# A DLRM tower on one core: the last group's layers in two halves, the weights in pieces, the third layer in two strips, and the pair moves shared out anew

## The chip, the cores and the metric

The kernel runs on 1 core of a Trainium2 chip. The metric is the time of one execution on the device in microseconds (us), as the median of the runs. Engines are named as the profile names them: PE is TensorE's matmuls and PEld its weight loads, DVE is VectorE, ACT ScalarE, POOL GpSimd and SP SyncE. SPq, ACTq and POOLq stand for DMA instructions that the engine issues.

## The reference, cut to what matters

A batch of 2048 rows. Each row looks up 27 embeddings of 128 floats in 27 tables, takes the inner product of every pair (351 of them), appends 16 dense inputs, and runs three dense layers (367 to 512 to 256 to 1).

```python
e = jnp.stack([tbl_0[ids[:, 0]], ..., tbl_26[ids[:, 26]]], axis=1)
xactions = jnp.einsum('bfd,bgd->bfg', e, e)
z = xactions[:, _TRIL_I, _TRIL_J].reshape(B, -1)
h = jnp.concatenate([z, dense_ctx], axis=1)
h = jnp.maximum(h @ W_top1 + b_top1, 0.0)
h = jnp.maximum(h @ W_top2 + b_top2, 0.0)
y = h @ W_top3
```

The tables have 1000, 1250, 12500 or 125000 rows. All arrays are float32.

## The kernel before

**Groups and tiles.** The batch is cut into 16 tiles of 128 rows, and two tiles make a group: 8 groups of 256 columns (`COLS`), numbered 0 to 7 (`LAST` is 7). In each group the embeddings come in two ways. The ten smallest tables ("hot") stay in SBUF, split into two float32r parts, and are looked up by matmuls with one-hot columns that DVE builds (L654; PE at L441 and L442, 180 matmuls a group). The other 17 tables ("cold") are gathered row by row by POOL's indirect DMAs (L402), one for each tile and table: 34 a group, 272 in all. PE transposes what they bring (L424, 17 a tile, in five batches of 4, 4, 4, 4 and 1). Both ways fill one of four PSUM banks `fill_ps`, and ACT moves each bank into `et` (cold L551, hot L563).

**Pairs.** For every row of the batch one small matmul (L458, 26x26, two instructions of PE each) gives the row's inner products. Four rows at a time lie in four column strips of PE. A group has four banks of 64 rows, `("pairs", g, 0)` to `("pairs", g, 3)`: banks 0 and 1 are its first tile, banks 2 and 3 its second. They alternate between two PSUM banks `pair_ps`, so bank n waits until bank n-2 has been moved out. `move_pairs` (L343) moves a bank with 16 copies: DVE takes strips 0 and 1 and ACT strips 2 and 3, so 8 copies each, and each engine counts what it moved on a semaphore of its own (`pair_moved_v`, `pair_moved_a`).

**z.** The copies put most pair products where the first layer reads them (`zt`, 3 chunks of 128 rows). Those of the 14 lower features and the dense inputs are placed by 15 small DMAs in `complete_zt` (L313, the dense one L309). In groups 0 to 6 SP issues all 15 after bank 3 of the group was moved.

**Layers.** layer1 (L471) is 12 matmuls of 256 columns, in 24 instructions of PE since a float32 matmul takes two; ACT applies bias and relu (L570). layer2 is 8 matmuls (L497, 16 instructions), in two halves m of 4, with relu at L575. layer3 is 2 matmuls with one weight column (L504); DVE copies the result to `y_row` (L661) and SP stores it (L363).

**Order.** `order()` (L77 to L92) lists the steps, and PE, ACT, DVE and SP each walk that list. For group g above 0, with b = g-1: the first hot fill, layer3 of b-1, pairs 2 and 3 of b among the hot fills, then the rest of the fills, layer1 of b, pairs 0 and 1 of g, and layer2 of b between them. So a group's layers run under the next group's fills. At a hot step DVE builds the one-hots of the hot step after it. At `("layer3", b)` DVE waits for PE and copies y, and SP waits for that copy, stores y and only then goes on to the next ids (`hot_ids`, L331) and to the next z.

**The end.** After the list there is nothing left to run under. PE runs 10 matmuls whose result is not used (`WARM`, L523), then `layer1_last` (L486) on 256 columns, chunk by chunk in the order 2, 1, 0, each chunk when its z has landed; of the last group's 15 moves SP issues 9 (chunk 2 first) and POOL 6. Then follow layer2, layer3, the y copy and the store.

**The start.** ACT issues the weights (L537, L538: 768 and 512 KB, and the vectors at L539) after it has moved group 0's last hot fill; the first layer waits for all three.

## Time and profile before

| what | us |
|---|---|
| median of 3 runs | 396.18 |
| lowest and highest of the 3 | 391.86 and 401.06 |
| the profiled execution, its own time | 398.12 |
| its span, first to last instruction | 396.2 |

The profile is of one execution: what it shows is read against 398.12, of which 1.9 lie around the span. A row of the timeline gives the start, the duration of the stretch, the engine, the line, the operation with its tiles and shapes and the count; in brackets stands how long the engine was idle before it and what ended that. The granted TensorE clock (PEclk) is 1.00 at 2.4 GHz and 0.50 at 1.2 GHz; its mean is 0.974 here.

### The profile page before, as it was taken

The page shows a single profiled execution, that of the slowest core. Times are in us where ns is not written, and L with a number is a line of the kernel's source. Part 1 is how long each engine was busy: PE and PEld are TensorE (multiplying, and loading weights), DVE is VectorE, ACT ScalarE, POOL GpSimd, SP SyncE. Part 2 cuts the span into 40 slices and gives each one's busy share as a digit, 9 for nine tenths or more (in the row PEclk, how much of TensorE's full clock was granted, in tenths as well). Part 3 has the DMA queues.
Part 4 walks back from the last instruction along what each step waited for, and adds up shares of the span by engine and source line. Part 5 has one row for each costly group of instructions (what it writes and reads, how often), then busy time and mean ns, then how long its engine had stood idle before and what let it go on. Part 6 is the DMA issues. An engine that isn't in the chain of part 4 may idle for free.

```text
span 396.2 us, 14625 instructions
## 1 busy us (share of the span) xinstructions
PE 353.3 (89%) x6180; PEld 321.6 (81%) x6180; DVE 264.3 (67%) x1044; ACT 212.2 (54%) x435; POOL 280.2 (71%) x286
## 2 busy tenths in 40 slices
PE   0876859999999969999999999999899999999677
PEld 0776849998789858998889888998799788997465
DVE  2999956992689454993779647992689457933310
ACT  3456273655647481563837483755447382746612
POOL 4887777777877777777777778777777777776030
PEclk9998968999999998999999999999999999999989
DMA  7984453224132522225232522234222422221000
GB/s 271 360 255 135 99 188 84 56 72 149 48 77 61 165 57 58 73 64 157 57 83 59 162 58 76 50 107 121 55 78 61 112 52 55 58 64 51 3 13 2
DMA packets 19602, 37.71 MB, mean 95 GB/s; under 512 B 6793, under 2 KB 8401, under 8 KB 19537
## 3 DMA queue, kind: packets, MB, share of 16 engines
q0 software_dynamic: 8896, 17.89, 17.2%
q1 hardware_dynamic: 8704, 16.00, 12.6%
q10 hardware_dynamic: 1936, 2.89, 2.2%
q8 instruction: 49, 0.80, 0.9%
q14 instruction: 17, 0.13, 0.1%
HBM read 35.88 MB, written 0.01 MB: 91 GB/s over the span
## 4 chain that ended last, share of the span: by engine, by line
PE 64%; POOL 16%; issue 7%; DMA 6%; SPq 3%; DVE 3%; ACT 2%; ACTq 0%
PE fill_ps L441 16%; PE fill_ps L442 16%; POOL rows L402 16%; PE pair_ps L458 10%; PE mlp_ps L471 7%; PE mlp_ps L497 6%; PE fill_ps L424 5%; DMA rows<-tbl_d,ids_sb 3%; SPq L313 3%; PE mlp_ps L504 2%; PE fill_ps L486 2%; DVE work L343 1%; DMA work<-work 1%; ACT et L551 1%; DMA ids_sb<-ids_d 1%
## 5 line engine op out<-in xcount | busy, mean ns | idle before, releaser
L402 POOL DMA_INDIRECT rows<-tbl_d,ids_sb x272 | 276.3, 1016 | 86.5 <-issue 80.2
L441 PE MATMUL fill_ps<-one_hot,table_hi 128*128 128x256 f32 x720 | 183.8, 294 | 14.1 <-DVE one_hot L654 14.1
L442 PE MATMUL fill_ps<-one_hot,table_lo 128*128 128x256 f32 x720 | 178.9, 288 | 0.0
L654 DVE TENSOR_SCALAR one_hot<-hot_ids 128x256 fp32r<-128x256 f32 x720 | 166.7, 303 | 13.1 <-PE fill_ps L442 12.3
L441 PEld LDWEIGHTS fill_ps<-one_hot,table_hi 128*128 128x128 f32 x720 | 141.8, 197 | 16.0 <-issue 14.0
L442 PEld LDWEIGHTS fill_ps<-one_hot,table_lo 128*128 128x128 f32 x720 | 141.9, 197 | 0.2
L343 DVE COPY work<-pair_ps 26x112 f32<-26x112 f32 (+1 forms) x256 | 66.0, 258 | 90.0 <-PE pair_ps L458 86.8
L343 ACT COPY work<-pair_ps 26x112 f32<-26x112 f32 (+1 forms) x256 | 61.2, 239 | 84.2 <-PE pair_ps L458 81.5
L551 ACT COPY et<-fill_ps 128x512 f32<-128x512 f32 (+1 forms) x80 | 79.4, 1118 | 0.5
L563 ACT COPY et<-fill_ps 128x512 f32<-128x512 f32 x40 | 46.7, 1225 | 41.4 <-PE fill_ps L442 34.4
L458 PEld LDWEIGHTS pair_ps<-et 128*26 128x26 f32 x4096 | 46.2, 104 | 25.4 <-issue 16.1
L458 PE MATMUL pair_ps<-et 128*26 128x26 f32 x4096 | 55.7, 193 | 12.0 <-issue 5.9
L424 PE MATMUL fill_ps<-ident,rows 128*128 128x128 f32 x272 | 39.5, 282 | 11.0 <-DMA rows<-tbl_d,ids_sb 10.9
L424 PEld LDWEIGHTS fill_ps<-ident,rows 128*128 128x128 f32 x272 | 30.8, 143 | 13.6 <-DMA rows<-tbl_d,ids_sb 12.9
L471 PE MATMUL mlp_ps<-work,w_sb 128*128 128x256 f32 x168 | 37.7, 381 | 1.5 <-DMA work<-work 0.9
L471 PEld LDWEIGHTS mlp_ps<-work,w_sb 128*128 128x128 f32 x168 | 31.4, 190 | 6.3 <-issue 1.3
L497 PE MATMUL mlp_ps<-work,w_sb 128*128 128x256 f32 x128 | 31.5, 392 | 0.0
L497 PEld LDWEIGHTS mlp_ps<-work,w_sb 128*128 128x128 f32 x128 | 24.2, 198 | 2.9
L570 ACT ACTIVATE work<-mlp_ps,vectors 128x256 f32<-128x256 f32 x28 | 11.8, 471 | 23.6 <-PE mlp_ps L471 23.6
L641 DVE TENSOR_SCALAR hot_ids<-hot_ids,first_row 128x512 f32<-128x512 int32 (+1 forms) x48 | 21.2, 455 | 4.0 <-DMA hot_ids<-ids_hot_d 4.0
L661 DVE COPY y_row<-mlp_ps 1x256 f32<-1x256 f32 x8 | 3.3, 412 | 19.6 <-PE mlp_ps L504 19.6
L544 ACT CAST table_hi<-work 128x1024 fp32r<-128x1024 f32 (+1 forms) x8 | 9.3, 1163 | 8.0 <-DMA work<-tbl_d 8.0
(22 smaller groups left out, 62.8 us busy)
## 6 DMA issues: line engine op xcount, KB each, us to landing
hot_ids<-ids_hot_d SPq DMA_DIRECT2D x34, 256.0 KB, 3.8
rows<-tbl_d,ids_sb POOLq DMA_INDIRECT x272, 2.5
work<-tbl_d SPq DMA_DIRECT2D x4, 640.0 KB, 4.3
work<-tbl_d SPq DMA_DIRECT2D x4, 512.0 KB, 7.1
hot_ids<-ids_hot_d ACTq DMA_DIRECT2D x6, 256.0 KB, 8.9
w_sb<-w_d ACTq DMA_DIRECT2D x1, 768.0 KB, 5.4
w_sb<-tbl_d SPq DMA_DIRECT2D x1, 640.0 KB, 4.1
w_sb<-tbl_d SPq DMA_DIRECT2D x1, 512.0 KB, 11.7
```

The source lines that it names most:

```text
L343: last = copy(pair_cols[STRIP * q:STRIP * q + PAIR_COLS, place(q + 1)[1]:, at:at + BANK_ROWS], frm[:, q::STRIPS, :])
L402: nc.gpsimd.indirect_dma_start(out=rows[:, t, c, :], out_offset=None, in_=tables[f], in_offset=bass.IndirectOffsetOnAxis(ap=ids_sb[:, tile ...
L424: last = nc.tensor.transpose(bank[:, c * P:(c + 1) * P], rows[:, t, c0 + c, :], ident[:, :])
L441: nc.tensor.matmul(to, table_hi[:, CHUNK_AT[k] + c, :], hot, start=(c == 0), stop=False)
L442: last = nc.tensor.matmul(to, table_lo[:, CHUNK_AT[k] + c, :], hot, start=False, stop=(c == CHUNKS_OF[k] - 1))
L458: last = nc.tensor.matmul(pair_ps[bank % 2][32 * s:32 * s + PAIR_COLS, r * PAIR_COLS:(r + 1) * PAIR_COLS], et[:, row, 0:FEATURES - 1], et[ ...
L471: last = nc.tensor.matmul(mlp_psum(m), w1_sb[:, c, m * P:(m + 1) * P], zt[:, c, :], start=(c == 0), stop=(c == CHUNKS - 1))
L497: last = nc.tensor.matmul(mlp_ps[m][:, 0:COLS], w2_sb[:, c, m * P:(m + 1) * P], h1[:, c, :], start=(c == 0), stop=(c == K2 - 1))
L551: nc.scalar.copy(et[:, t * P:(t + 1) * P, c0:c0 + n].rearrange("p r f -> p f r"), fill_ps[FILL[step] % FILL_RING][:, 0:n * P].rearrange("p ...
L563: nc.scalar.copy(et[:, :, slot:slot + n].rearrange("p r f -> p f r"), fill_ps[FILL[step] % FILL_RING][:, 0:n * COLS].rearrange("p (f r) -> ...
L641: nc.vector.tensor_scalar(ids.bitcast(F32), ids, first_row[:, n:n + 1], None, ALU.subtract).then_inc(hot_ids_local, 1)
L654: last = nc.vector.tensor_scalar(one_hot[:, (first + c - c0) % ONE_HOT_RING, :], ids, float(c), None, ALU.is_equal)
```

## The change

Five edits:

1. **The last group in two halves.** The layers of group 7 run for its first tile (128 columns) and then for its second. z of the first tile is placed as soon as its banks 0 and 1 are moved, 8 moves issued by SP and 7 by POOL; z of the second after bank 3, 5 moves each by SP, POOL and ACT (`lows_by`). PE's order is layer1 of half 0, layer2 of half 0, layer1 of half 1, layer3 of half 0, layer2 and layer3 of half 1. The 10 unused matmuls go.
2. **Order at the end.** The second half of layer2 of group 6 comes after bank 2 of group 7, no longer before it; layer3 of group 6 comes after bank 3.
3. **Weights in pieces and later.** w1 is loaded in 3 pieces after the first three cold fills of tile 1 of group 0, w2 in 2 pieces, and the vectors, after hot fills 2 and 3 of group 1.
4. **layer3 in two strips** for groups 0 to 6: 4 matmuls of 128 columns, written to two column strips of PE, and two y copies of 128 columns. DVE makes them after it has moved bank 3 of the next group, no longer at the step `layer3`. SP's store stays where it was in its list, ahead of that group's z.
5. **Pair moves.** In groups 0 to 6 ACT moves all of bank 2 (16 copies) and DVE none of it. In group 7 DVE moves all of bank 1 and ACT none. Waits on moved banks count with `moved_through`.

The diff, cut to its core:

```diff
             steps += hot[4:] + cold[0][4:] + [("layer1", b), ("pairs", g, 0)] + cold[1][:2]
-            steps += [("layer2", b, 0), ("pairs", g, 1)] + cold[1][2:] + [("layer2", b, 1)]
-    return steps + [("pairs", GROUPS - 1, 2), ("layer3", GROUPS - 2), ("pairs", GROUPS - 1, 3)]
+            steps += [("layer2", b, 0), ("pairs", g, 1)] + cold[1][2:]
+            if g < LAST:
+                steps.append(("layer2", b, 1))
+    return steps + [("pairs", LAST, 2), ("layer2", LAST - 1, 1), ("pairs", LAST, 3), ("layer3", LAST - 1)]
...
+def strips_of(engine, g, bank):
+    alone = {("dve", 1): range(STRIPS), ("act", 1): range(0)} if g == LAST else {
+        ("act", 2): range(STRIPS), ("dve", 2): range(0)}
+    shared = range(2) if engine == "dve" else range(2, STRIPS)
+    return tuple(alone.get((engine, bank), shared))
...
+def lows_by(engine, t):
+    movers = (("sp", "pool"), ("sp", "pool", "act"))[t]
+    return ALL_LOWS[movers.index(engine)::len(movers)]
...
-        y_ps = mlp_ps[0][0:1, COLS:2 * COLS]
+        y_ps = [mlp_ps[0][STRIP * t:STRIP * t + 1, COLS:COLS + P] for t in range(GROUP_TILES)]
+        y_last_ps = [pair_ps[t][0:1, 0:P] for t in range(GROUP_TILES)]
...
 (SP)
+                elif step == ("pairs", LAST, 1):
+                    complete_zt(sp, LAST, 0, P, lows_by("sp", 0), z_last_in[0])
+                elif step == ("pairs", LAST, PAIR_BANKS - 1):
+                    complete_zt(sp, LAST, P, COLS, lows_by("sp", 1), z_last_in[1])
                 elif step[0] == "layer3":
                     store(step[1])
-            complete_zt(sp, LAST, lows_of(2), z_last_in[2])
-            complete_zt(sp, LAST, SP_LAST_0, z_in)
...
 (PE)
+            def layer1_last(t):
+                pe.wait_ge(z_last_in[t], 16 * (Z_MOVES - len(lows_by("pool", t))))
+                pe.wait_ge(z_last_by_pool[t], 16 * len(lows_by("pool", t)))
+                for m in range(K2):
+                    for c in range(CHUNKS):
+                        last = nc.tensor.matmul(fill_ps[m][:, t * P:(t + 1) * P], w1_sb[:, c, m * P:(m + 1) * P],
+                                                zt[:, c, t * P:(t + 1) * P], start=(c == 0), stop=(c == CHUNKS - 1))
+                    last.then_inc(h1_full, 1)
...
             def layer3(g):
                 for c in range(M2):
                     pe.wait_ge(h2_done, g * M2 + c + 1)
-                    last = nc.tensor.matmul(y_ps, w3_sb[:, c:c + 1], h2[:, c, :],
+                    for t in range(GROUP_TILES):
+                        last = nc.tensor.matmul(y_ps[t], w3_sb[:, c:c + 1], h2[:, c, t * P:(t + 1) * P],
+                                                start=(c == 0), stop=(c == M2 - 1))
...
-            for _ in range(WARM):
-                nc.tensor.matmul(mlp_ps[1][:, 0:COLS], w2_sb[:, 0, 0:P], h1[:, 0, :], start=True, stop=True)
-            layer1_last()
+            pe.wait_ge(fill_moved, len(FILL))
+            layer1_last(0)
             pe.wait_ge(y_done, LAST)
-            for m in range(M2):
-                layer2(LAST, m)
-            layer3(LAST)
+            layer2_last(0)
+            layer1_last(1)
+            layer3_last(0)
+            layer2_last(1)
+            layer3_last(1)
...
 (ACT)
-            def load_weights():
-                act.wait_ge(lo_made, MOST_HOT)
-                act.dma_start(w1_sb[:, :, :], w1.rearrange("(c p) n -> p c n", p=P)).then_inc(w_in, 16)
-                act.dma_start(w2_sb[:, :, :], w2.rearrange("(c p) n -> p c n", p=P)).then_inc(w_in, 16)
+            def load_weights(step):
+                if step[0] == "cold" and step[1:3] == (0, 1) and step[3] < CHUNKS:
+                    c = step[3]
+                    act.wait_ge(lo_made, MOST_HOT)
+                    act.dma_start(w1_sb[:, c, :], w1[c * P:(c + 1) * P, :]).then_inc(w_in, 16)
+                elif step in (("hot", 1, 2), ("hot", 1, 3)):
+                    c = K2 // 2 * (step[2] - 2)
+                    act.dma_start(w2_sb[:, c:c + K2 // 2, :], ...).then_inc(w_in, 16)
...
 (DVE)
                     move_pairs(dve, g, bank, strips_of("dve", g, bank), pair_moved_v, nc.vector.tensor_copy)
-                elif step[0] == "layer3":
-                    output(step[1])
-            output(LAST)
+                    if bank == PAIR_BANKS - 1 and g > 0:
+                        output(g - 1)
+            dve.wait_ge(stored, 16 * LAST)
+            for t in range(GROUP_TILES):
+                output_last(t)
```

How the instructions stand now, at three places. First PE at the end of the program, before the change, from the last batch of transposes on (`mlp_ps<-work,w_sb` with 128x256 is layer2 at L497, the unused matmuls at L523; `fill_ps<-work,w_sb` is layer1):

```order
L424 MATMUL fill_ps<-ident,rows 128x128 x9
L497 MATMUL mlp_ps<-work,w_sb 128x256 x4
L458 MATMUL pair_ps<-et 26x26 x64
L504 MATMUL mlp_ps<-work,vectors 1x256 x2
L458 MATMUL pair_ps<-et 26x26 x64
L523 MATMUL mlp_ps<-work,w_sb 128x256 x10
L486 MATMUL fill_ps<-work,w_sb 128x256 x12
L497 MATMUL mlp_ps<-work,w_sb 128x256 x8
L504 MATMUL mlp_ps<-work,vectors 1x256 x2
```

And after it (L444 transposes, L477 pairs, L508 layer2, L525 layer3 of group 6, L500 layer1 of a half, L517 layer2 of a half, L533 layer3 of a half):

```order
L444 MATMUL fill_ps<-ident,rows 128x128 x9
L477 MATMUL pair_ps<-et 26x26 x64
L508 MATMUL mlp_ps<-work,w_sb 128x256 x4
L477 MATMUL pair_ps<-et 26x26 x64
L525 MATMUL mlp_ps<-work,vectors 1x128 x4
L500 MATMUL fill_ps<-work,w_sb 128x128 x12
L517 MATMUL mlp_ps<-work,w_sb 128x128 x8
L500 MATMUL fill_ps<-work,w_sb 128x128 x12
L533 MATMUL pair_ps<-work,vectors 1x128 x2
L517 MATMUL mlp_ps<-work,w_sb 128x128 x8
L533 MATMUL pair_ps<-work,vectors 1x128 x2
```

Bank 2's pairs now follow the transposes directly, layer2 of group 6 stands between the last two banks, and the layers of group 7 stand twice at half the width.

Second, ACT at the end, after the change, from the last cold fills on (L587 cold fills, L614 relu of layer2 of group 6, L361 pair moves, L609 and L619 relus of the halves):

```order
L587 COPY et<-fill_ps 128x4x128 x2
L587 COPY et<-fill_ps 128x128
L361 COPY work<-pair_ps 26x7x16 x2
L361 COPY work<-pair_ps 26x6x16 x2
L361 COPY work<-pair_ps 26x7x16 x2
L361 COPY work<-pair_ps 26x6x16 x2
L614 ACTIVATE work<-mlp_ps,vectors 128x256
...
L329 DMA work<-work 12x128
L325 DMA work<-dense_d 16x128
L609 ACTIVATE work<-fill_ps,vectors 128x128 x4
L619 ACTIVATE work<-mlp_ps,vectors 128x128 x2
```

Before the change eight moves of bank 1 (L343) stood ahead of those cold fills; now ACT goes from the relu of layer2 straight to them. It issues five DMAs ahead of the relus of half 0.

Third, DVE in a middle group, before the change, from the y copy on (L654 one-hots, L641 ids made local, L343 pair moves):

```order
L661 COPY y_row<-mlp_ps 1x256
L343 COPY work<-pair_ps 26x7x16 x2
L343 COPY work<-pair_ps 26x6x16 x2
L343 COPY work<-pair_ps 26x7x16 x2
L343 COPY work<-pair_ps 26x6x16 x2
L654 TENSOR_SCALAR one_hot<-hot_ids 128x256 x8
L641 TENSOR_SCALAR hot_ids<-hot_ids,first_row 128x512
L654 TENSOR_SCALAR one_hot<-hot_ids 128x256 x10
L343 COPY work<-pair_ps 26x7x16 x2
```

And after it (L703 one-hots, L690 ids, L361 moves, L710 and L711 y copies):

```order
L703 TENSOR_SCALAR one_hot<-hot_ids 128x256 x16
L690 TENSOR_SCALAR hot_ids<-hot_ids,first_row 128x512
L703 TENSOR_SCALAR one_hot<-hot_ids 128x256 x10
L361 COPY work<-pair_ps 26x7x16 x2
L361 COPY work<-pair_ps 26x6x16 x2
L361 COPY work<-pair_ps 26x7x16 x2
L361 COPY work<-pair_ps 26x6x16 x2
L710 COPY y_row<-mlp_ps 1x128
L711 COPY y_row<-mlp_ps 1x128
```

The moves of bank 2 and the y copy are gone from ahead of the one-hots, and two y copies stand behind bank 3's moves.

## Rows read from the trace of the kernel before

**Rows 1.** Waits of POOL: engine, line, waited for, us in total, times, longest.
```profile
POOL rows L402 <- issue: 80.2, 263, 0.3
POOL rows L402 <- PE fill_ps L424: 2.4, 8, 0.3
```

**Rows 2.** The view of line L402, the gathers: min/median/max ns, first and last start.
```profile
L402 POOL DMA_INDIRECT rows<-tbl_d,ids_sb x272: 940/947/2475, 5.6 to 363.5; - x136
```

**Rows 3.** Waits of PE from 58 to 376.
```profile
PE fill_ps L424 <- DMA rows<-tbl_d,ids_sb: 7.2, 7, 1.6
```

**Rows 4.** Timeline of a middle group (group 4, z of group 3), PE, SP and DVE.
```profile
204.82 1.82 PE L458 MATMUL pair_ps<-et 128*26 128x26 f32 x128
222.72 5.42 PE L471 MATMUL mlp_ps<-work,w_sb 128*128 128x256 f32 x24
...
200.02 0.35 SPq L331 DMA_DIRECT2D hot_ids<-ids_hot_d  x1
210.19 4.89 SPq L313 DMA_DIRECT2D work<-work  x7
...
220.57 0.53 SPq L309 DMA_DIRECT2D work<-dense_d  x1
...
208.01 2.15 DVE L343 COPY work<-pair_ps 26x112 f32<-26x112 f32 x8
```

**Rows 5.** Timeline of PE at the start, banks of group 0.
```profile
54.35 1.75 PE L458 MATMUL pair_ps<-et 128*26 128x26 f32 x119 [4.00 <-issue]
...
57.99 0.90 PE L424 MATMUL fill_ps<-ident,rows 128*128 128x128 f32 x3 [0.84 <-DMA rows<-tbl_d,ids_sb]
```

**Rows 6.** DMA queues from 50.1 to 51.8 (q10, ACT's), then from 51.8 to 54.4 (q8, instructions): packets, MB, share.
```profile
q10 hardware_dynamic: 524, 0.63, 101.7%
...
q8 instruction: 1, 0.02, 2.9%
```

**Rows 7.** GB/s from 372 to 375 in 40 slices; its one packet is q8's.
```profile
GB/s 0 0 218 0 0 0 0 0 0 0 0 0 0 0 0 0 0 0 0 0 0 0 0 0 0 0 0 0 0 0 0 0 0 0 0 0 0 0 0 0
```

**Rows 8.** Timeline of PE at the end.
```profile
367.33 0.33 PE L424 MATMUL fill_ps<-ident,rows 128*128 128x128 f32 x1 [1.31 <-DMA rows<-tbl_d,ids_sb]
...
370.75 1.24 PE L458 MATMUL pair_ps<-et 128*26 128x26 f32 x126 [1.36 <-ACT et L551]
...
374.89 0.92 PE L458 MATMUL pair_ps<-et 128*26 128x26 f32 x87 [1.72 <-issue]
...
382.51 7.10 PE L486 MATMUL fill_ps<-work,w_sb 128*128 128x256 f32 x24 [2.19 <-DMA work<-work]
```

**Rows 9.** Timeline of ACT, then DVE, at the end.
```profile
366.25 1.99 ACT L343 COPY work<-pair_ps 26x112 f32<-26x112 f32 x8
368.26 2.44 ACT L551 COPY et<-fill_ps 128x512 f32<-128x512 f32 x3
...
388.36 1.77 ACT L570 ACTIVATE work<-fill_ps,vectors 128x256 f32<-128x256 f32 x4 [10.50 <-PE fill_ps L486]
...
365.05 2.15 DVE L343 COPY work<-pair_ps 26x112 f32<-26x112 f32 x8 [1.14 <-PE pair_ps L458]
...
375.87 2.15 DVE L343 COPY work<-pair_ps 26x112 f32<-26x112 f32 x8 [1.20 <-PE pair_ps L458]
394.26 0.41 DVE L661 COPY y_row<-mlp_ps 1x256 f32<-1x256 f32 x1 [16.25 <-PE mlp_ps L504]
```

**Rows 10.** Timeline of SP, then POOL, at the end: issues of the last z.
```profile
378.05 6.14 SPq L313 DMA_DIRECT2D work<-work  x8
...
378.49 3.08 POOL L313 DMA_DIRECT2D work<-work  x6 [14.06 <-DVE work L343]
```

**Rows 11.** One stretch at the start, two at the end: us, busy (and count) of PE, PEld, DVE, ACT, POOL, then PEclk, DMA share, GB/s.
```profile
58.00:62.80 4.80, 4.80 (x23) 4.80 (x24) 3.01 (x13) 2.82 (x5) 3.83 (x4) 0.50 0.22 58
...
380.31:383.72 3.41, 1.22 (x7) 1.11 (x7) 0.00 (x0) 0.00 (x0) 1.26 (x3) 1.00 0.08 17
383.72:387.13 3.41, 3.41 (x10) 2.70 (x9) 0.00 (x0) 0.00 (x0) 0.00 (x0) 0.50 0.06 13
```

More of the change, by code:

```diff
@@ L52 @@
 GROUPS = TILES // GROUP_TILES
+LAST = GROUPS - 1
 STRIPS = 4
@@ L64 @@
 RAW_SLOTS = 4
-WARM = 10
 def hot_fills(g):
@@ L107, with moved_through @@
 NEXT_HOT = {a: b for a, b in zip(list(HOT_FILL), list(HOT_FILL)[1:])}
+def strips_of(engine, g, bank):
[3 more added lines that the diff above has]
+    return tuple(alone.get((engine, bank), shared))
+def moved_through(engine, number):
+    return sum(1 for _, g, bank in list(BANK)[:max(number, 0)] if strips_of(engine, g, bank))
 def halves(k):
@@ L161 @@
 M2 = HIDDEN2 // P
-MOVES = HIGH - 1
+Z_MOVES = HIGH
 def place(i):
@@ L190 @@
 ALL_LOWS = list(range(1, HIGH)) + [0]
-def lows_of(chunk):
-    return [low for low in ALL_LOWS if HOMES[low][1] == chunk]
-LAST_ORDER = [2, 1, 0]
-POOL_LAST_0, SP_LAST_0 = lows_of(0)[:2], lows_of(0)[2:]
+def lows_by(engine, t):
+    movers = (("sp", "pool"), ("sp", "pool", "act"))[t]
+    return ALL_LOWS[movers.index(engine)::len(movers)]
 def contraction_rows():
@@ L285, in build @@
         z_in = sem("z_in")
-        z_last_in = [sem(f"z_last_in{c}") for c in range(CHUNKS)]
-        dense_in = sem("dense_in")
+        z_last_in = [sem(f"z_last_in{t}") for t in range(GROUP_TILES)]
+        z_last_by_pool = [sem(f"z_last_by_pool{t}") for t in range(GROUP_TILES)]
         w_in = sem("w_in")
@@ L335, in move_pairs @@
         def move_pairs(engine, g, bank, strips, moved, copy):
+            if not strips:
+                return
             engine.wait_ge(pair_full, BANK["pairs", g, bank] + 1)
@@ L499, in layer2, with layer2_last @@
                 last.then_inc(h2_full, 1)
+            def layer2_last(t):
+                for m in range(M2):
+                    for c in range(K2):
+                        if m == 0:
+                            pe.wait_ge(h1_done, (LAST + t) * K2 + c + 1)
+                        last = nc.tensor.matmul(mlp_ps[m][:, t * P:(t + 1) * P], w2_sb[:, c, m * P:(m + 1) * P],
+                                                h1[:, c, t * P:(t + 1) * P], start=(c == 0), stop=(c == K2 - 1))
+                    last.then_inc(h2_full, 1)
             def layer3(g):
@@ L582, in pairs @@
                         act.wait_ge(zt_clear, 1)
-                    wait_count(act, z_in, g * (16 * MOVES))
-                move_pairs(act, g, bank, (2, 3), pair_moved_a, nc.scalar.copy)
+                    wait_count(act, z_in, g * (16 * Z_MOVES))
+                move_pairs(act, g, bank, strips_of("act", g, bank), pair_moved_a, nc.scalar.copy)
             early = []
@@ L614, in _ @@
                     relu2(step[1], step[2])
+            complete_zt(act, LAST, P, COLS, lows_by("act", 1), z_last_in[1])
             for m in range(K2):
-                relu1(LAST, m)
+                relu1_last(0, m)
             for m in range(M2):
-                relu2(LAST, m)
+                relu2_last(0, m)
+            for m in range(K2):
+                relu1_last(1, m)
+            for m in range(M2):
+                relu2_last(1, m)
         @block.vector
```

85 lines of the change are left out of this document (45 added, 40 removed).

## The prediction

> **What bounds the kernel now.** I read the waits of POOL first, then those of PE, then the timeline at three places: a middle group, the start and the end. The chain of waits names PE for most of the span, and that misleads. POOL issues 272 gathers and is idle before each for 0.3 us of "issue", never longer, even where PE had to free the buffer [rows 1]. So its stream runs unblocked from 5.6 to 363.5, at a median of 0.947 + 0.3 = 1.25 us a gather [rows 2]. PE waits for such rows seven times between 58 and 376, 7.2 us together [rows 3], the last time at 367.33, for the very last gather, after 1.31 us of idling [rows 8]. Whatever makes PE faster before 367.33 ends in a longer wait there. Of what comes after, 29 us to the span's end, nothing lies under gathers: there the change can give time.
>
> A second chain is just as long as PE's in the middle. In group 4 PE ends the pairs of bank 3 at 204.82 + 1.82 = 206.64. DVE moves them only from 208.01, since one-hots are ahead, SP starts z at 210.19 and issues the last move at 220.57, and layer1 starts at 222.72, 2.15 after that issue [rows 4]. So z is late by about nothing, and has no slack either.
>
> **The change part by part, from the last gather on.**
>
> *Bank 2 earlier.* PE starts it at 370.75, after 1.36 us of waiting for ACT's cold fills [rows 8]. ACT spends 366.25 to 368.24 on its half of bank 1 and only then 2.44 us on three cold fills [rows 9]. With bank 1 left to DVE the fills run from 366.25 and end at 368.7. Bank 2 starts at 368.7: -2.05. DVE's 16 copies of bank 1 take 2 x 2.15 from 365.05 [rows 9], to 369.35; bank 3 comes later than that.
>
> *Between bank 2 and bank 3.* Before, layer3 stood there (4 instructions) and PE then stopped 1.72 us for "issue" in the middle of bank 3 [rows 8]. The only packet that any queue moves from 372 to 375 is one of instructions, at 372.15 to 372.22 [rows 7]. I read the stop as a wait for instructions: two banks of 256 instructions close together use them up faster than they come. At the start the same stop lasts 4.00 us, to 54.35 [rows 5]: from 50.1 to 51.8 ACT's queue, the weights, fills the DMA engines (101.7%), and the packet of instructions comes only after 51.8 [rows 6]. Now layer2 (8 instructions) stands between: at 5.42 / 24 = 0.225 us each [rows 4] that is 1.8 instead of 0.9 us. The stop shrinks by the difference to about 0.8. Bank 3 then ends at 368.7 + 1.24 + 1.8 + 1.24 + 0.8 = 373.8, against 375.8. With the stop at nothing it is 373.0, at full length 374.7.
>
> The Trainium skill ("Runtime: NRT & Kernel Launch", Instruction fetch mechanics) speaks against this reading: it says that the sequencer fetches the next page while it executes the current one, and that this is hidden. By that rule the stop would have another cause and stay 1.72, and the sum would be 0.9 us longer. The trace does not bear it out in bursts of pairs, and the trace decides.
>
> *Half 1's z.* The moves of bank 3 take 2.15: all is moved at 376.0, against 378.02. SP takes 6.14 / 8 = 0.77 us an issue and POOL 3.08 / 6 = 0.51 [rows 10]. Before, SP's fourth issue (the last of chunk 2) started at 378.05 + 3 x 0.77 = 380.35 and PE started 2.15 later. Now the fifth starts at 379.1, and PE may start half 1 at 381.3. What ACT takes for an issue of this kind no row shows: POOL's 0.51 and SP's 0.77 bound it; I take 0.6, and the five end at 379.0 (378.6 to 379.9).
>
> *Half 0.* SP issues its 8 from 369.4, the last at 374.8; PE can start at 377.0. Its 24 instructions are half as wide, 0.11 each: 2.7, to 379.7. ACT's relus are queued behind its DMAs, from 379.0. A relu of 256 columns takes 1.77 / 4 = 0.44 in a row [rows 9]; at 128 it lies between 0.22 and 0.44, I take 0.33, and four end at 380.3. What is left of layer2 then takes about 1.1, to 381.4: half 0 and z of half 1 come together.
>
> *Half 1's layers.* layer1 2.7 to 384.1, layer3 of half 0 0.5, layer2 1.8 to 386.4, relu 0.45, layer3 0.5: DVE copies y at 387.4. Before it did at 394.26 [rows 9]. That is -6.9.
>
> *The clock.* PE was busy for 1.22 us of the 3.41 from 380.31 on, and in the next 3.41 the granted clock was 0.50, 1.2 GHz; layer1 took 7.10 instead of 5.42 [rows 8, 11]. Now PE idles from 374.2 to 377.0 and the 20 unused instructions are gone, so one such stretch is likely, earlier or later. Lying on half 0 alone it costs nothing or 1, on half 1 1.7. I take 1.0. The y copy moves to 388.4: -5.9.
>
> *The start.* With no weights in the way the stop at 54.35 falls from 4.00 towards the 1.72 of the end. But PE then waits for rows that land at 57.99 anyway [rows 5], and behind these stand the waits of [rows 3]. Price 0; if gathers did not bound, up to 2.3. The last half of w2 is issued some 4 us before layer1 of group 0; a delay of 1 us there goes into a wait for rows.
>
> *The middle.* DVE is rid of 2.15 us of moves and so free when bank 3 is full: it moves from 206.65 instead of 208.01, to 208.8. Then come two y copies; 128 columns cost between 0.2 and the 0.41 of 256 [rows 9], I take 0.3. SP waits for them, since its store stands ahead of z, and behind the store an issue of ids of 0.35 [rows 4] is queued. z starts at 208.8 + 0.6 + 0.3 + 0.35 = 210.05, against 210.19. Price 0 (-0.3 to +0.2 a group). ACT's 8 more copies take 2.0 us [rows 9] of the time in which it waits between the two banks. layer3 in two strips is between 0.4 us saved and 0.3 lost a group, under the gathers.
>
> The sum: 398.12 - 5.9 = 392.2 for an execution like the profiled one. That one stood 1.9 over the median of 396.18, so I forecast 396.18 - 5.9 = 390.3.
>
> **The rivals.**
>
> *A. PE bounds in the timed runs.* Gathers of up to 2475 ns [rows 2] can make the profiled stream slow; in a run like the 391.86 one PE might be the bound. Then the start counts too: 2.3 for the stop, and 2.4 for the stretch from 58 to 62.8, all of it at half the clock [rows 11]. That gives 390.3 - 4.7 = 385.6. Against it: seven waits for rows.
>
> *B. The store holds z back.* If DVE is not free at 206.65, because the ring of 20 one-hots makes it wait for PE, it moves at 208.01 as before and z starts at 210.16 + 1.25 = 211.4, 1.2 late in each of seven groups. Of 8.4 us some 1.3 go into the last wait for rows: 390.3 + 7.1 = 397.4, slower than before. It decides from about 1.0 us of lateness a group (7 x 1.0 = 5.9 + 1.3). For it: z has no slack at all. Against it: ACT, which has no one-hots, moves at once when the bank is full.
>
> *C. The clock takes back the end.* If the three stretches of layers mostly run at 1.2 GHz, layer1 and layer2 of half 1 take up to 4.5 more: 3.5 above what the sum has, 393.8. For it: 20 matmuls that kept PE busy are gone. Against it: after its one slow stretch before, the clock was back.
>
> **How the numbers follow.** Forecast 0.52, A 0.18, B 0.12, C 0.18. The forecast's own range is 388 to 393: 0.9 either way for the stop, 0.9 for ACT's issues, 1.0 for the clock, and the three runs of before spread by 9 us, so a median is good to 2 or so. With A and the nearer part of B the range is 385.3 to 396.6. About 2% is what a measurement of this kernel tells from no change: 388.3 to 404.1. Faster: A 0.16 and 0.12 of the forecast, 0.28. Slower: the far end of B, 0.04. Within 2%: 0.68.
>
> **What would show it.** Right: POOL's last gather near 363.5 again with 0.3 of issue before each; bank 2 about 1.4 us after the last transposes; all z of half 1 issued within 4 us; the y copy about 21 us after the last transpose instead of 27; z's first issue 3.4 us after the pairs of bank 3 in middle groups. Wrong: waits of layer1 for z or w2 in most groups (B), a granted clock of 0.50 over more than one stretch behind 377 (C), or waits for rows that vanish while the end moves ahead (A).

## The result and the profile after

| what | kernel before | changed kernel |
|---|---|---|
| median, us (4 runs each, taken together) | 398.62 | 442.98 |
| lowest and highest | 391.86 and 406.94 | 437.08 and 450.64 |
| ratio of the two, 95% interval | | 1.114 (1.082 to 1.146) |
| the profiled execution and its span | 398.12, 396.2 | 440.47, 438.6 |

The ratio leaves out executions over 1.5% above the fastest of their kernel (the two slowest of each here), so it is not the quotient of the medians.

The change costs 11%; 390.3 was forecast. The view of the gathers' line, the waits of POOL and those of PE, after (the counterparts of [rows 1 to 3]):

```profile
L422 POOL DMA_INDIRECT rows<-tbl_d,ids_sb x272: 940/945/9577, 4.6 to 409.9; - x136
```

```profile
POOL rows L422 <- issue: 80.8, 265, 0.3
POOL rows L422 <- PE fill_ps L444: 1.5, 5, 0.3
```

```profile
PE fill_ps L444 <- DMA rows<-tbl_d,ids_sb: 45.3, 18, 9.3
```

POOL still waits for nothing but its 0.3 of issue, the median gather is still 0.945, and yet the last gather starts 46.4 us later than in [rows 2], and PE waits 9.3 us at a stretch for rows. The longest gather went from 2.475 to 9.577 us. The costliest group of the page, before and then after (busy us, mean ns of one, idle before):

```profile
L402 POOL DMA_INDIRECT rows<-tbl_d,ids_sb x272 | 276.3, 1016 | 86.5 <-issue 80.2
```

```profile
L422 POOL DMA_INDIRECT rows<-tbl_d,ids_sb x272 | 323.7, 1190 | 85.6 <-issue 80.8
```

The spans differ by 42.4. The gathers take 47.4 more, the idle time before them 0.9 less, and what follows the start of the last gather is 28.7 (438.6 - 409.9) instead of 32.7: 47.4 - 0.9 - 4.0 = 42.5. So the whole loss is the gathers' own duration. It is six of them, one a group from the fills of group 2 on; three in the timeline of POOL, after (the others start at 225.64, 275.95 and 330.12 and take 9.40 to 9.48):

```profile
117.10 9.55 POOL L422 DMA_INDIRECT rows<-tbl_d,ids_sb  x1 [0.30 <-issue]
...
171.38 9.58 POOL L422 DMA_INDIRECT rows<-tbl_d,ids_sb  x1 [0.30 <-issue]
...
380.45 9.18 POOL L422 DMA_INDIRECT rows<-tbl_d,ids_sb  x1 [0.30 <-issue]
```

Each is some 8.5 us over the median, 51 us in all, a little more than the 47.4. No other gather after the start takes over 1.2 us but one of 3.28 at 104.54; the kernel before has two of 2.48 and 2.47. What DVE does meanwhile, timeline after:

```profile
116.40 0.28 DVE L710 COPY y_row<-mlp_ps 1x128 f32<-1x128 f32 x1
116.69 0.28 DVE L711 COPY y_row<-mlp_ps 1x128 f32<-1x128 f32 x1
116.90 2.09 DVE L703 TENSOR_SCALAR one_hot<-hot_ids 128x256 fp32r<-128x256 f32 x10
118.92 0.47 DVE L690 TENSOR_SCALAR hot_ids<-hot_ids,first_row 128x512 f32<-128x512 int32 x1
119.31 4.11 DVE L703 TENSOR_SCALAR one_hot<-hot_ids 128x256 fp32r<-128x256 f32 x20
123.35 0.47 DVE L690 TENSOR_SCALAR hot_ids<-hot_ids,first_row 128x512 f32<-128x512 int32 x1
123.74 2.09 DVE L703 TENSOR_SCALAR one_hot<-hot_ids 128x256 fp32r<-128x256 f32 x10
```

and the same place in the kernel before, DVE and then POOL:

```profile
117.98 1.60 DVE L343 COPY work<-pair_ps 26x96 f32<-26x96 f32 x6
119.61 2.23 DVE L654 TENSOR_SCALAR one_hot<-hot_ids 128x256 fp32r<-128x256 f32 x10
121.76 0.54 DVE L641 TENSOR_SCALAR hot_ids<-hot_ids,first_row 128x512 f32<-128x512 int32 x1
122.22 4.46 DVE L654 TENSOR_SCALAR one_hot<-hot_ids 128x256 fp32r<-128x256 f32 x20
...
119.76 0.97 POOL L402 DMA_INDIRECT rows<-tbl_d,ids_sb  x1 [0.30 <-issue]
121.03 1.02 POOL L402 DMA_INDIRECT rows<-tbl_d,ids_sb  x1 [0.30 <-issue]
```

Two things are to be seen. Before, 20 one-hots take 4.46 us and gathers of 1.02 run beside them; after, 20 take 4.11 and one gather stands from 117.10 until 126.65, 0.82 after DVE's stream ended at 125.83. POOL is served in the first case and not in the second. And before, the moves end at 119.58 and the one-hots start at 119.61, 0.03 later; after, the last y copy ends at 116.97 and the one-hots have started at 116.90, 0.07 ahead of that.

The theories put to the test: T1, the two y copies directly ahead of the long run of one-hots shut a gather out; T2, the relief of DVE in bank 2 shifts one-hots against gathers; T3, SP's store ahead of z's moves is at fault.

### The profile page after: what moved, and what is told of

The parts are those of the page before. It is cut to its first block, busy times and chain, and to the rows that moved or that the text cites. A ratio compares the mean times of both kernels' runs of the same rounds, so it can differ in the third digit from the quotient of the medians.

```text
span 438.6 us, 14764 instructions
## 1 busy us (share of the span) xinstructions
PE 363.2 (83%) x6232; PEld 333.0 (76%) x6232; DVE 250.0 (57%) x1004; ACT 226.1 (52%) x489; POOL 330.5 (75%) x292
## 3 DMA queue, kind: packets, MB, share of 16 engines
q10 hardware_dynamic: 2076, 2.91, 2.2%
## 4 chain that ended last, share of the span: by engine, by line
POOL 44%; PE 31%; issue 12%; DMA 7%; SPq 2%; ACTq 1%; DVE 1%; ACT 1%; POOLq 0%
POOL rows L422 44%; DMA rows<-tbl_d,ids_sb 6%; PE mlp_ps L489 6%; PE fill_ps L461 6%; PE fill_ps L462 6%; PE pair_ps L477 5%; PE fill_ps L444 3%; PE mlp_ps L508 3%; SPq L329 2%; PE mlp_ps L517 1%; ACTq L329 1%; DMA ids_sb<-ids_d 1%; DVE work L361 1%; PE fill_ps L500 1%; DMA work<-dense_d 1%
## 5 line engine op out<-in xcount | busy, mean ns | idle before, releaser
L422 POOL DMA_INDIRECT rows<-tbl_d,ids_sb x272 | 323.7, 1190 | 85.6 <-issue 80.8
L703 DVE TENSOR_SCALAR one_hot<-hot_ids 128x256 fp32r<-128x256 f32 x720 | 163.8, 295 | 77.3 <-PE fill_ps L462 76.4
L461 PE MATMUL fill_ps<-one_hot,table_hi 128*128 128x256 f32 x720 | 189.4, 300 | 14.6 <-DVE one_hot L703 14.5
L462 PE MATMUL fill_ps<-one_hot,table_lo 128*128 128x256 f32 x720 | 184.1, 293 | 0.0
L461 PEld LDWEIGHTS fill_ps<-one_hot,table_hi 128*128 128x128 f32 x720 | 146.3, 203 | 16.0 <-issue 12.4
L462 PEld LDWEIGHTS fill_ps<-one_hot,table_lo 128*128 128x128 f32 x720 | 146.1, 203 | 0.3
L361 ACT COPY work<-pair_ps 26x112 f32<-26x112 f32 (+1 forms) x304 | 72.4, 238 | 71.1 <-PE pair_ps L477 67.8
L361 DVE COPY work<-pair_ps 26x112 f32<-26x112 f32 x208 | 53.6, 258 | 87.8 <-PE pair_ps L477 85.3
L587 ACT COPY et<-fill_ps 128x512 f32<-128x512 f32 (+1 forms) x80 | 80.2, 1101 | 28.4 <-PE fill_ps L444 27.9
L444 PE MATMUL fill_ps<-ident,rows 128*128 128x128 f32 x272 | 45.3, 303 | 45.3 <-DMA rows<-tbl_d,ids_sb 45.3
L444 PEld LDWEIGHTS fill_ps<-ident,rows 128*128 128x128 f32 x272 | 33.1, 152 | 50.6 <-DMA rows<-tbl_d,ids_sb 49.9
L477 PEld LDWEIGHTS pair_ps<-et 128*26 128x26 f32 x4096 | 45.0, 104 | 17.8 <-issue 10.9
L477 PE MATMUL pair_ps<-et 128*26 128x26 f32 x4096 | 53.4, 193 | 6.0 <-ACT et L599 1.3
L489 PE MATMUL mlp_ps<-work,w_sb 128*128 128x256 f32 x168 | 39.4, 393 | 3.5 <-DMA work<-dense_d 3.5
L508 PE MATMUL mlp_ps<-work,w_sb 128*128 128x256 f32 x112 | 33.2, 450 | 0.0
L508 PEld LDWEIGHTS mlp_ps<-work,w_sb 128*128 128x128 f32 x112 | 25.1, 236 | 3.8
L690 DVE TENSOR_SCALAR hot_ids<-hot_ids,first_row 128x512 f32<-128x512 int32 (+1 forms) x48 | 20.7, 445 | 4.1 <-DMA hot_ids<-ids_hot_d 4.1
L680 DVE TENSOR_TENSOR table_lo<-work,table_hi 128x1024 fp32r<-128x1024 f32 (+1 forms) x8 | 10.8, 1345 | 2.4 <-ACT table_hi L580 2.4
```

The costliest lines, as they stand in the source:

```text
L361: last = copy(pair_cols[STRIP * q:STRIP * q + PAIR_COLS, place(q + 1)[1]:, at:at + BANK_ROWS], frm[:, q::STRIPS, :])
L422: nc.gpsimd.indirect_dma_start(out=rows[:, t, c, :], out_offset=None, in_=tables[f], in_offset=bass.IndirectOffsetOnAxis(ap=ids_sb[:, tile ...
L444: last = nc.tensor.transpose(bank[:, c * P:(c + 1) * P], rows[:, t, c0 + c, :], ident[:, :])
L461: nc.tensor.matmul(to, table_hi[:, CHUNK_AT[k] + c, :], hot, start=(c == 0), stop=False)
L462: last = nc.tensor.matmul(to, table_lo[:, CHUNK_AT[k] + c, :], hot, start=False, stop=(c == CHUNKS_OF[k] - 1))
L477: last = nc.tensor.matmul(pair_ps[bank % 2][32 * s:32 * s + PAIR_COLS, r * PAIR_COLS:(r + 1) * PAIR_COLS], et[:, row, 0:FEATURES - 1], et[ ...
```

## The experiments

They ran on five chips, the kernel before timed beside them on each; a time without a count of runs is one execution. On two of the chips it took 394.64 and 395.92 us; on the other three 604.53, 600.10 and 606.73. Those three are told of apart below ("the slow chips"): there the gathers' durations can be read, but the time is set by something else.

**The y copies back.** The changed kernel with one edit:

```diff
                     if bank == PAIR_BANKS - 1 and g > 0:
-                        output(g - 1)
+                elif step[0] == "layer3":
+                    output(step[1])
```

> The changed kernel with the two y copies of the middle groups back where the kernel before has them, ahead of the last layer's activation reads. T1 (the contiguous y copies directly ahead of a long run of one-hots shut a gather of GpSimd out until the run ends; six gathers of 9.2 to 9.6 us cost about 50 us): no gather over 4 us after the start, mean of L422 back from 1190 to about 1020 ns, and on a chip where the kernel before takes about 398 us this one takes 388 to 394 us. T2 (the relief of VectorE in bank 2's moves shifts one-hots against gathers): the long gathers stay and the time is about 440 us. T3 (SyncE's store right ahead of z's moves is at fault): the same, about 440 us, since the store still goes out ahead of z.

394.74 us (10 runs) against 394.64, ratio 0.9994 (0.9947 to 1.0041). Its page and line view (from 60 us on):

```profile
L422 POOL DMA_INDIRECT rows<-tbl_d,ids_sb x272 | 277.3, 1019 | 85.7 <-issue 80.2
```

```profile
L422 POOL DMA_INDIRECT rows<-tbl_d,ids_sb x235: 940/947/1749, 59.7 to 363.7; - x118
```

No gather over 1.75 us, and the last starts at 363.7 again. Against 442.98 of the changed kernel the 11% hang on the place of two copies of 0.28 us. The time is 0.7 us above the range expected of T1. T2 falls: the shares are as in the changed kernel. T3 does not fall here, against what I expected of this run: SP waits for the y copies, so its store moved with them, from 0.8 us ahead of z's first move (117.00 and 117.78) to 8.9 us ahead (108.68 and 117.60). The next run tells.

**The store behind z.** The changed kernel, SP's side alone:

```diff
+                    if step[1] > 0:
+                        store(step[1] - 1)
...
-                elif step[0] == "layer3":
+                elif step[0] == "layer3" and step[1] == LAST - 1:
```

> The changed kernel with SyncE's store of the group before issued behind z's moves instead of ahead of them in the middle groups; nothing on VectorE changes. T1: six gathers of 9 to 9.6 us stay and the time stays at 435 to 445 us. T3 (the store makes z late and the gathers long): no long gather, about 390 us.

437.24 us, six gathers of 9.0 to 9.6. T3 falls.

**One copy added to the kernel before.** Nothing is moved; behind bank 3's moves DVE makes one more copy, which nothing reads, in groups 1 to 6:

```diff
+            if extra:
+                last = copy(spare[0:1, 0:P], pair_ps[bank % 2][0:1, 0:P])
             last.then_inc(moved, 1)
...
+                               extra=bank == PAIR_BANKS - 1 and 0 < g < LAST)
```

> The kernel before, nothing moved, with one extra copy of 1 x 128 elements (contiguous on both sides, from PSUM to a spare tile that nothing reads) on VectorE behind bank 3's moves in groups 1 to 6. T1: five or six gathers of 7 to 9.6 us, one a group, and a time of 425 to 445 us, though the copy itself takes under 0.3 us. T2 and T3 (neither the shares nor the store is changed here): no long gather, time of the kernel before within 2 us.

442.69 us: a copy of 0.28 us a group costs 48 us. The effect needs no part of the change. Is it the form of the copy? Three more forms in its place: read strided; written strided; and 26 partitions, exactly as a pair move.

> As the run with the extra contiguous copy, but the extra copy reads PSUM and writes its tile in the interleaved pattern of the pair moves (1 partition, 8 x 16). If the form of the copy decides (pair moves in this pattern stand ahead of the one-hots in the kernel before without any long gather): no long gather, time of the kernel before within 2 us. If any extra instruction between the pair moves and the one-hots does it (its place or a shift by 0.2 us): five or six gathers of 7 to 9.6 us and 425 to 445 us.

> As the run before, but the extra copy has one partition only, with the same 7 x 16 strided write. If it is the strided write that keeps GpSimd served: no long gather, 390 to 398 us. If it is the number of partitions or the place: six long gathers, 437 to 445 us.

> The kernel before with one extra copy behind bank 3's moves in groups 1 to 6, this time in the form of the pair moves themselves: 26 partitions, 7 x 16 elements, both sides strided. If the form of the last instruction ahead of the one-hots decides (the pair moves end 0.03 us before the first one-hot starts, the copies on one partition end 0.07 us after it): no long gather, the time of the kernel before within 2 us, about 390 to 398. If any further instruction there does it: a gather of 9 to 10.6 us in each of six groups, 437 to 445 us.

444.14, 444.81 and 437.02 us, with six gathers of 9.3 to 10.6, 9.4 to 10.6 and 7.1 to 9.3 us. I had thought that the form decides, and it does not: all four forms of the copy do it. The last of the three shows that it need not be the next gather that is shut out. DVE and then POOL in it:

```profile
120.84 0.26 DVE L347 COPY spare<-pair_ps 26x112 f32<-26x112 f32 x1
121.03 2.36 DVE L659 TENSOR_SCALAR one_hot<-hot_ids 128x256 fp32r<-128x256 f32 x10
123.32 0.46 DVE L646 TENSOR_SCALAR hot_ids<-hot_ids,first_row 128x512 f32<-128x512 int32 x1
123.71 4.12 DVE L659 TENSOR_SCALAR one_hot<-hot_ids 128x256 fp32r<-128x256 f32 x20
127.75 0.47 DVE L646 TENSOR_SCALAR hot_ids<-hot_ids,first_row 128x512 f32<-128x512 int32 x1
128.15 3.84 DVE L659 TENSOR_SCALAR one_hot<-hot_ids 128x256 fp32r<-128x256 f32 x18
...
121.01 0.95 POOL L407 DMA_INDIRECT rows<-tbl_d,ids_sb  x1 [0.30 <-issue]
122.26 1.02 POOL L407 DMA_INDIRECT rows<-tbl_d,ids_sb  x1 [0.30 <-issue]
123.59 8.29 POOL L407 DMA_INDIRECT rows<-tbl_d,ids_sb  x1 [0.30 <-issue]
```

Two gathers are served, the first of them started 0.02 us before the first one-hot, and the third, which starts while DVE makes ids local, is shut out; so it goes in five of the six groups. That third gather ends at 131.88, while DVE's stream goes on to 131.99 and beyond without a gap: it got in without one.

What all four have in common is that the copy ends after the first one-hot has started (121.10 against 121.03 here): the short gap of 0.03 that stood there is gone. The ten profiles of chips of about 395 us have 70 runs of 30 or more DVE instructions behind a copy, counted from 60 us on. In 34 the copy ends 0.03 us ahead of the first one-hot, and no gather in them takes over 1.14 us, whether the first one starts 0.78 us before the run or 0.19 after its start. In 36 it ends 0.07 after that start, and each of these has one gather of 7.1 to 10.6 us. The changed kernel has both kinds: its run at 74.11, behind the moves of group 0, which has no y copy ahead, has the gap and no long gather. So it is not the moment at which a gather starts.

**The y copies ahead of the moves.** The changed kernel, so that pair moves stand before the one-hots again:

```diff
+                    if bank == PAIR_BANKS - 1 and 0 < g < LAST:
+                        output(g - 1)
                     move_pairs(dve, g, bank, strips_of("dve", g, bank), pair_moved_v, nc.vector.tensor_copy)
-                    if bank == PAIR_BANKS - 1 and g > 0:
+                    if bank == PAIR_BANKS - 1 and g == LAST:
                         output(g - 1)
```

> The changed kernel with the two y copies ahead of bank 3's pair moves in the middle groups instead of behind them, so that pair moves stand directly ahead of the one-hots. T1: no gather over 4 us after the start, 388 to 395 us, as with the y copies back where the kernel before has them. If the place of the y copies anywhere near the run is enough: long gathers stay and the time is above 430 us.

390.73 us (4 runs, 389.02 to 400.38) against 395.92 (7 runs), ratio 0.985 (0.977 to 0.993): a gain of 1.5%, which is outside the interval of this measurement and under the 2% from which a kernel is called faster. The changed kernel itself was not timed on this chip. DVE and the gathers (line view from 60 us on) in it:

```profile
115.28 2.16 DVE L361 COPY work<-pair_ps 26x112 f32<-26x112 f32 x8
117.47 2.26 DVE L703 TENSOR_SCALAR one_hot<-hot_ids 128x256 fp32r<-128x256 f32 x10
...
L422 POOL DMA_INDIRECT rows<-tbl_d,ids_sb x234: 943/948/1158, 59.8 to 360.1; - x117
```

The gap of 0.03 is back (117.44 to 117.47), and no gather takes over 1.16 us. Beside it ran the kernel before once more, for a profile.

> The kernel before, unchanged, for a profile of the same chip: no long gather but one or two of 2.5 us; the stretch from the last gather's start to the end 32.7 us as in its first profile, against about 29 in the changed kernel with the y copies back.

392.12 us, span 390.2, no gather over 1.14 from 60 us on, last gather at 360.5 and 29.7 us to the end. My 32.7 did not come back: the stretch after the last gather itself varies by 3 us in the kernel before. Half of that is layer1, which took 5.65 us there at a granted clock of 1.00 against the 7.10 of [rows 8]. On this chip the two profiles differ by 0.8 us behind the last gather's start, 29.7 against 28.9.

**Gaps put into the stream.** Now the y copies stay where the change put them, and DVE waits for its own one-hots, which makes a gap of 0.03 us; after each of the twelve parts behind the y copies, or, with `since[0] == 4`, only after the fourth:

```diff
                     last.then_inc(hot_made, 1)
+                    since[0] += 1
+                    if since[0] <= 12:
+                        dve.wait_ge(hot_made, part + 1)
...
                         output(g - 1)
+                        since[0] = 0
```

Both times they fell on chips where the kernel before takes 600 us.

> The changed kernel, y copies where it has them, but VectorE waits for its own count of finished one-hots after each of the first twelve parts behind the y copies, so that the stream of one-hots has a short gap every 4 or 5 instructions. If a gather waits for a gap in VectorE's stream: no gather over about 2.5 us and 390 to 400 us. If it waits for something else (the DMA queue, the landing of rows): six gathers above 9 us and 437 to 445 us.

> As the run before with only one such wait in each group, after the fourth part (16 to 20 one-hots behind the y copies, about 4 us into the run). If a gather waits for a gap: six gathers of 4 to 5 us instead of 9.5, or a long one after it in the second half; time 405 to 425 us. If it is the time since the y copies or anything else: six gathers of about 9.5 us and 437 to 445 us.

With a gap after each part: 590.26 against 600.10 us, and one gather over 2.5 us behind 60 us (3.44 at 132, at a place where each of the ten profiles of such chips has one). With one gap: 592.94 us, and five gathers of 2.91 beside that one. The changed kernel without gaps never ran on such a chip; the kernel before with the extra copy has five of 7.0 to 7.3 there (below). DVE and POOL with the one gap, in narrow windows:

```profile
191.76 0.48 DVE L705 TENSOR_SCALAR one_hot<-hot_ids 128x256 fp32r<-128x256 f32 x2
...
192.27 0.29 DVE L705 TENSOR_SCALAR one_hot<-hot_ids 128x256 fp32r<-128x256 f32 x1
...
190.15 2.91 POOL L422 DMA_INDIRECT rows<-tbl_d,ids_sb  x1 [14.66 <-PE fill_ps L444]
193.37 1.03 POOL L422 DMA_INDIRECT rows<-tbl_d,ids_sb  x1 [0.30 <-issue]
```

Ten one-hots pass, at 192.24 to 192.27 DVE has its gap of 0.03, and the gather that stood since 190.15 ends at 193.06, 0.82 after it (as 0.82 after the stream's end in the changed kernel): a little less than a whole gather of 0.94. I read it so that the gather had waited for that gap and did nearly all of its work behind it. All ten gathers of this kind, five in each of the two runs with one gap, end 0.82 or 0.83 after the start of the gap. That a gap is the only way in is not so: of the 36 long gathers on the chips of 395 us 23 end 0.82 or 0.83 after DVE's stream stops, if only for 0.03, and 13 end within the stream or 0.13 after its end, so they got in while it ran. What let them in no row shows. Both kernels with gaps ran again, on a third chip of the slow kind.

> The changed kernel with a wait of VectorE for its own one-hots after each of the twelve parts behind the y copies, again, on a chip where the kernel before takes about 395 us (the run before this fell on one where it takes 600). If a gather waits for a gap in VectorE's stream: no gather over 2.5 us after the start and 388 to 398 us. If it waits for something else: six gathers above 9 us and 437 to 445 us.

> As the run before with one such wait in each group, after the fourth part, again on the same chip. If a gather waits for a gap: six gathers of 3 to 5 us in place of 9.5, and the time follows their sum: 405 to 420 us. If it waits for anything else: six of about 9.5 us and 437 to 445 us.

583.06 against 606.73 us, ratio 0.963 (0.956 to 0.971), again with a single gather of 3.44 behind 60 us; and 605.94 us, with five of 2.85 to 2.92. With a gap after each part no gather over 3.44 us is left on either chip; that it gives the 50 us back where they cost them was not measured.

**The slow chips.** Four kernels ran on the first of them; three come here, the fourth further down.

> The changed kernel with one thing undone: DVE makes the two y copies at the step layer3 again, ahead of bank 2, and no longer between bank 3's moves and the one-hots; all else of the change stays. Theory 1 (the y copies directly ahead of a long run of one-hots shut POOL's gathers out): none of the six gathers of 9.2 to 9.6 us is left, which is 6 x 8.3 = 50 us, and the time falls from 443 to 388 to 394. Theory 2 (it is DVE's relief of bank 2, by which the one-hots fall at other times against the gathers): the long gathers stay, 435 to 445. Theory 3 (SP's store right ahead of z's moves): the store now comes 10 us before z, so this too says 388 to 394; another run has to tell it from theory 1.

> The kernel before with one thing done: DVE's one y copy of 256 columns comes behind the moves of bank 3, ahead of the one-hots. Theory 1: six gathers of 9 us or more, and a time of 435 to 450. Theory 2: no such gather, 393 to 402.

> The kernel before with one more DVE copy in each of the groups 1 to 6, directly behind the 8 moves of bank 3: 1 x 128 floats in a row of PSUM into a spare tile that nothing reads. The y copy stays where it is, and SP's order too. Theory 1: the copy alone brings the six long gathers, 435 to 450. Theories 2 and 3: nothing changes beyond 0.3 us a group, 394 to 402.

602.52 (ratio 1.0007, 0.9943 to 1.0072), 610.39 and 609.09 us against 604.53: the y copies back have no gather over 4 us behind the start (four of 3.4 and two of 2.4), a single y copy moved in the kernel before has five of 7.2 to 7.8, the extra copy five of 7.0 to 7.3. As to which of these three have long gathers, T1 holds; the time hardly shows it. The same kernel, the one with the y copies back, the waits of PE's weight loads and of POOL, first at 602.52, then at 394.74 us:

```profile
PEld pair_ps L477 <- issue: 95.0, 116, 2.0
...
POOL rows L422 <- PE fill_ps L444: 156.9, 20, 15.6
POOL rows L422 <- issue: 74.7, 245, 0.3
```

```profile
PEld pair_ps L477 <- issue: 8.5, 37, 0.5
...
POOL rows L422 <- issue: 80.2, 263, 0.3
```

On the slow chip PE's weight loads idle 95 us with nothing that the profile shows them to wait for ("issue"), the mean granted clock is 0.80 against 0.97, and POOL waits 157 us for PE. The gathers have that much slack and no longer set the time, so a long one costs little. I take the 95 us for late instructions, as I did with the stop at the start, but no run shows it: both pages have the same 49 packets of instructions (0.80 MB). Why three chips of the five are so stays open.

The other runs there price the rest.

> The kernel before with the new shares of the pair moves alone (bank 2 all on ACT, the last group's bank 1 all on DVE). Theory 1: no gather over 3 us after the start, 392 to 402. Theory 2: gathers of 9 us in every group, 435 to 450.

> The kernel before with the new shares of pair moves alone (ScalarE all of bank 2 in groups 0 to 6, VectorE all of bank 1 in group 7). By the prediction's steps bank 2 of the last group comes 2 us earlier and the middle gains nothing: 392 to 397 us, ratio 0.99 to 1.0. T2 (the relief of VectorE in bank 2's moves shuts gathers out): long gathers and over 430 us.

> The changed kernel with the y copies ahead of bank 3's pair moves, measured again in more rounds: the run of it before gave a ratio of 0.985 with an interval of 0.977 to 0.993. Expected 388 to 393 us and a ratio between 0.98 and 0.995: all terms of the prediction's sum but the gathers then hold (390.3 was forecast).

The shares alone took 593.04 us (one run) against 604.53 on the first chip and 591.80 (4 runs) against 600.10 on the second, ratio 0.987 (0.981 to 0.992), with no gather over 3.5 us. On these chips they gain over 1%; on the others they were not run. The y copies ahead gave 600.80 against 600.10, ratio 1.000 (0.997 to 1.003), and there this order is no cure: four gathers of 6.8 us and one of 2.35 beside the one of 3.44. On such a chip a gather starts after a wait of 14.9 us for PE, 2.3 us into DVE's run, so POOL stood still when the run began; the gap ahead of the run does not help it. The kernel with a gap after each part gained 3.7% on one of those chips; on the other its single run of 590.26 lies among the four of the shares alone (589.73 to 594.0), so which is better there is open.

## Why the prediction was wrong

**The step that failed** is "The middle", with the sentence that it rests on, that POOL's "stream runs unblocked". Of the two y copies I priced what they take on DVE (0.3 each; measured 0.28) and what is queued behind them on DVE and SP, and came to "Price 0 (-0.3 to +0.2 a group)". What they do to a gather on another engine, with which they share no semaphore, was no term at all: I took 1.25 us a gather as a constant. It measured 9.2 to 9.6 for one gather a group, six times, +47.4 us in all. The range of that step should have been open above, since [rows 2] had gathers of 2.475 us in it; I used them only in rival A, to make the stream faster.

The Trainium skill ("SBUF — State Buffer", Who interferes with whom, and The "DVE blocks DMA" trap in SBUF: two separate sides) would have named it: a DMA issued from GpSimd needs a port that VectorE's faster modes hold, `tensor_scalar` can run in one, and the engine that comes second is blocked outright. The trace agrees in that a gather does not share with DVE: 20 one-hots take 4.11 us while a gather is stopped, and 4.46 with gathers served, each of which comes with one longer one-hot. That it is this port no run here shows. The trace differs in the length: the page has the loser wait for the end of the one instruction, and here a gather stood through some 40 of 0.27 us each, 9.5 us. Each starts 0.07 before the one ahead ends, but that alone does not shut a gather out: in the kernel before they overlap by 0.08, and gathers are served.

Point by point:

- *The stream of the gathers sets the time before 367.* Right, and more than I made of it: 47.4 us of gathers became 42.4 us of span.
- *z in the middle.* Right. After, DVE moves bank 3 as soon as it is full, at 222.61 (8 copies to 224.77), and z starts at 226.17, 3.56 behind the full bank against the 3.4 forecast. Rival B, the store that holds z back, did not come: layer1 waits for z 3 times, 3.5 us in all, against once and 0.9 before.
- *The start.* The stop fell from 4.00 [rows 5] to 0.98, and PE then waited 3.08 for rows instead. That the price was 0, as forecast, fits: what PE gained it waited.

```profile
51.39 1.71 PE L477 MATMUL pair_ps<-et 128*26 128x26 f32 x119 [0.98 <-issue]
...
56.75 1.33 PE L444 MATMUL fill_ps<-ident,rows 128*128 128x128 f32 x5 [3.08 <-DMA rows<-tbl_d,ids_sb]
```

- *The end.* 4.0 us from the last gather's start on against 5.9 forecast, and the 4.0 flatter it: the y copy, for which 21 us behind the last transposes were forecast instead of 27, came after 24.3 (436.80 - 412.48), so 2.6 us are the end's own; 1.3 come from the rows of the last gather, which PE took up 2.6 us after that gather's start instead of 3.8. The last transposes, bank 2, bank 3 and half 0 in the timeline after, PE, then ACT, then DVE's last y copy:

```profile
412.48 0.47 PE L444 MATMUL fill_ps<-ident,rows 128*128 128x128 f32 x1 [0.23 <-DMA rows<-tbl_d,ids_sb]
413.76 1.76 PE L477 MATMUL pair_ps<-et 128*26 128x26 f32 x128 [0.81 <-ACT et L587]
415.46 3.06 PE L508 MATMUL mlp_ps<-work,w_sb 128*128 128x256 f32 x8
418.45 1.24 PE L477 MATMUL pair_ps<-et 128*26 128x26 f32 x126
...
420.05 2.94 PE L500 MATMUL fill_ps<-work,w_sb 128*128 128x128 f32 x24
...
427.05 3.07 PE L517 MATMUL mlp_ps<-work,w_sb 128*128 128x128 f32 x16 [4.06 <-ACT work L609]
...
421.95 3.73 ACTq L329 DMA_DIRECT2D work<-work  x4
...
426.54 1.14 ACT L609 ACTIVATE work<-fill_ps,vectors 128x128 f32<-128x128 f32 x4 [4.78 <-issue]
...
436.80 0.28 DVE L715 COPY y_row<-pair_ps 1x128 f32<-1x128 f32 x1 [2.47 <-PE pair_ps L533]
```

  Bank 2 starts 1.28 us behind the start of the last transposes, at 412.48 (1.4 forecast). No stop is left in bank 3, where I kept 0.8 and the other reading 1.72; but layer2 ahead of it took 3.06 us instead of 1.8, so the size of that term was not put to the test. Layer1 of half 0 starts 0.36 us behind bank 3, where I had 3.2. But ACT takes 3.73 / 4 = 0.93 us an issue, over both bounds that I had (0.51 and 0.77); its five take 4.5 instead of 3.0, its relus come that much later, and PE waits 4.06 for them. That term was mis-sized: 0.6 taken, 0.93 measured, and all z of half 1 took 4.5 us to issue, not 4. It is the same without long gathers: 0.93 an issue, and PE waits 2.56 us for these relus with the y copies back and 3.63 with them ahead.
- *The clock.* Two stretches at 0.50 from the last gather on, where one was forecast; the first covers bank 2 and two thirds of layer2 of group 6. The last row is of the y copies ahead:

```profile
407.40:417.60 10.20, 5.93 (x141) 4.43 (x140) 4.64 (x19) 4.50 (x11) 6.40 (x10) 0.50 0.13 33
417.60:427.90 10.30, 6.24 (x171) 5.44 (x171) 2.74 (x11) 3.53 (x13) 2.49 (x5) 1.00 0.04 8
427.90:431.30 3.40, 3.40 (x18) 3.40 (x18) 0.00 (x0) 0.74 (x2) 0.00 (x0) 0.50 0.03 5
...
363.57:370.40 6.83, 5.64 (x160) 4.40 (x164) 3.84 (x15) 3.23 (x11) 3.58 (x7) 0.50 0.06 11
```

  That the first comes from the long gathers is not shown: such a stretch stands at bank 2 without them too, with the y copies ahead (last row) and with them back (3.41 us from 368.12). Before the second PE was busy for 6.24 of 10.30 us and had just waited 4.06 for ACT. Only that second one lies behind the start of half 0, for which the prediction had 377, so the sign of rival C, more than one stretch behind it, did not come.

**What the rest of the change is worth.** Without the long gathers it measured 0.9994 (y copies back) and 0.985 (y copies ahead), on two chips, against the 0.985 that 390.3 stands for. In their profiles the first has 277.3 us of gathers and the second 273.9, and 29.3 and 28.9 from the last gather on; that is 3.8 of the 4.0 between their spans. The second agrees with the forecast, the first does not. The shares of the pair moves alone gave 0.987 on a slow chip, where the whole change with the y copies back gave 1.0007; why is open. And since the kernel before itself had 276.3 and 273.3 us of gathers in two profiles, and 32.7 and 29.7 from the last gather's start to its end, a gain of 5.9 is neither shown nor excluded.

## What to carry to other kernels

Where GpSimd issues indirect DMAs beside a long stream of short VectorE instructions like these one-hots, the time of one DMA issue is no constant: it can last for most of the stream, and here a copy of 0.28 us that closed a gap of 0.03 cost 8 us. Look at the maximum of such a group and not only at its median, and ask of every edit on VectorE which gaps it closes. A wait of VectorE for its own last result is a cheap way to make one: here it took the long gathers away, on chips where they cost little.

## What the hardware showed beside that

- A gather that is served beside the stream goes with one one-hot that lasts 0.40 us instead of 0.28, and the stream goes on. Behind a gap all gathers of the run are served, and it looks as if the first drew the others in. But with the extra copy in the form of a pair move two were served and the third was shut out in five groups of six. Why one is shut out and the next served stays open; the four forms of the extra copy and the y copies had a long gather in six groups of six, the orders with pair moves ahead in none on the chips of 395 us.
- The same kernel took 394.74 us on one chip and 602.52 on another, with 95 us instead of 8.5 of unexplained idling before PE's weight loads of the pairs; three chips of the five used in the experiments were of that kind, and a change of order was worth 1.5% on the one kind and nothing on the other.
